# A transformer block with routed experts: thirteen filling products in each attention-only body of TensorE's program

## The reference, cut to what matters

```python
h = patches(x) @ W.T + b                       # 32 x 196 x 192
h = concatenate([h, txt], axis=1)              # 32 x 324 x 192
h = h + causal_attention_one_head_rope(layernorm(h), Wq, Wk, Wv)
n = layernorm(h)
y = n + proj(attention_12_heads(layernorm(n) * w + b))
logits = (layernorm(y) * w2 + b2) @ w_gate     # 8 experts, best 2 of them, softmax of the two
out = h + y + sum_over_experts(gate * (gelu(xn2 @ W1 + b1) @ W2 + b2))
```

## Time and profile before

| | |
|---|---|
| median of 3 runs | 2925.34 us (2924.81 to 2934.8) |
| the profiled execution | 2913.08 us |
| its span, first to last instruction | 2911.2 us |
| mean granted TensorE clock | 0.892 of full speed |
| PE busy | 2480.0 us, 85% of the span |
| VectorE busy | 1634.7 us, 56% |
| ScalarE busy | 1203.2 us, 41% |
| GpSimd busy | 785.4 us, 27% |

### The profile page before, as it was taken

How to read it: one execution, slowest core, us unless ns; L and a number is a source line. 1 busy time by engine, 2 the same in 40 slices (tenths; PEclk the granted TensorE clock), 3 DMA queues, 4 the chain that set the end, 5 groups by cost and what they waited for, 6 DMA issues and landing times.

```text
span 2911.2 us, 62705 instructions
## 1 busy us (share of the span) xinstructions
PE 2480.0 (85%) x19692; PEld 1930.7 (66%) x19692; DVE 1634.7 (56%) x3896; ACT 1203.2 (41%) x2270; POOL 785.4 (27%) x1003
## 2 busy tenths in 40 slices
PE   3888999999999998999999999999976788888600
PEld 3856666666666666777777777777756777777500
DVE  2358778887877877666666666666642111111133
ACT  2223343344334333565666666566652323333200
POOL 1113223323333332222222222222211121211265
PEclk9669789898989988999999999999999989889855
DMA  6513112211311224244444444444333666766533
GB/s 117 143 18 46 28 28 44 41 28 33 52 28 28 48 37 113 63 115 114 113 105 105 105 105 105 108 107 110 96 110 124 217 225 211 232 208 208 162 110 96
DMA packets 267172, 297.50 MB, mean 102 GB/s; under 512 B 36156, under 2 KB 235304, under 8 KB 267112
## 3 DMA queue, kind: packets, MB, share of 16 engines
q1 hardware_dynamic: 248680, 264.80, 36.4%
q0 software_dynamic: 18432, 31.93, 3.8%
HBM read 236.04 MB, written 60.55 MB: 102 GB/s over the span
## 4 chain that ended last, share of the span: by engine, by line
PE 72%; issue 7%; DVE 7%; DMA 5%; POOL 3%; ACT 3%; SPq 2%; DVEq 0%; ACTq 0%; POOLq 0%
PE PS L1590 45%; PE PS L1734 7%; PE PS L1745 6%; DMA B2t<-in_L_ffn_b 4%; PE PS L1661 3%; PE PS L1711 3%; POOL pool L826 2%; DVE MX L1258 2%; PE PS L1784 1%; DVE rsi L1270 1%; PE PS L1622 1%; PE PS L1672 1%; ACT XE L988 1%; ACT pool L968 1%; DMA pool<-ybuf,ydst 1%
## 5 line engine op out<-in xcount | busy, mean ns | idle before, releaser
L1258 DVE TENSOR_REDUCE MX<-PS 108x2 f32<-108x648 f32 x576 | 460.6, 825 | 87.0 <-PE PS L1711 81.0
L968 ACT ACTIVATE pool<-PS 108x648 f32<-108x648 f32 x576 | 389.9, 711 | 217.1 <-PE PS L1734 178.6
L1590 PE MATMUL PS<-WB,big 128*128 128x192 f32 x2304 | 428.8, 343 | 2.6 <-ACT big L997 2.6
L1590 PE MATMUL PS<-XE,WF 128*128 128x256 f16 x2880 | 365.9, 281 | 56.9 <-ACT XE L988 46.6
L1590 PEld LDWEIGHTS PS<-WB,big 128*128 128x128 f32 x2304 | 397.9, 201 | 17.2 <-issue 10.0
L997 ACT ACTIVATE big<-PS,WF 128x256 f32<-128x256 f32 x576 | 241.5, 470 | 361.6 <-PE PS L1590 360.9
L1590 PEld LDWEIGHTS PS<-XE,WF 128*128 128x128 f16 x2880 | 277.2, 100 | 122.6 <-ACT big L997 40.8
L1402 DVE TENSOR_TENSOR big<-PS,B2t 128x384 f32<-128x384 f32 x96 | 53.5, 557 | 530.2 <-PE PS L1590 530.1
L826 POOL DMA_INDIRECT pool<-ybuf,ydst x192 | 193.7, 1009 | 481.7 <-DVE pool L1425 321.1
L814 POOL DMA_INDIRECT xbuf<-XH,DST x192 | 192.4, 1002 | 230.6 <-DVE DST L1340 169.1
L1270 DVE RECIPROCAL rsi<-rsi 128x324 f32<-128x324 f32 x96 | 209.1, 2178 | 3.3
(11 more groups left out here) (207 smaller groups left out, 4254.3 us busy)
## 6 DMA issues: line engine op xcount, KB each, us to landing
WF<-w1p SPq DMA_DIRECT2D x96, 771.0 KB, 4.7
WB<-in_L_ffn_W SPq DMA_DIRECT2D x96, 576.0 KB, 5.7
ximg<-in_x SPq DMA_DIRECT2D x96, 196.0 KB, 5.0
ximg<-in_x SPq DMA_DIRECT2D x96, 195.1 KB, 8.4
Xt<-xbuf SPq DMA_DIRECT2D x96, 192.0 KB, 2.5
ybuf<-big SPq DMA_DIRECT2D x96, 192.0 KB, 5.8
B2t<-in_L_ffn_b SPq DMA_DIRECT2D x96, 96.0 KB, 6.0
rbuf<-RP SPq DMA_DIRECT2D x32, 248.1 KB
```

The lines of the kernel that those rows point to most:

```text
L968: nc.scalar.activation(Pr[:, at:at + 2, :], pair(("st", p))[0:TP, :, 0:T], ACT.Exp, scale=SCALE2).then_inc(S["ex"], 1)
L1258: nc.vector.tensor_reduce(MX[:, qt, g, 64 * jj:64 * jj + 64:32], pair(("s", p))[0:TP, :, 0:T], AX.X, ALU.max).then_inc(S["mx"], 1)
L1590: last = nc.tensor.matmul(out_ap, lhsT, rhs, start=(i == 0), stop=(i == len(products) - 1))
```

## The change

Each ATTEND body gets 13 more matmuls on PE, whose results nobody reads: 5 before `s1`, 3 before `pj`, 5 before `tr2`. Each has the 128 by 128 identity in fp16 as its weights and 512 columns of the first image weights (`attWa`, fp16) as the moving operand, and writes the first bank of the pair that the step is about to write. For that, the wait for the bank now comes first, then the fill, then the wait for the data. In BOTH bodies the two waits of these steps change places too, and nothing is filled. `tr1` stays as it was.

```diff
+            FILL = {("s1",): 5, ("pj",): 3, ("tr2",): 5}
+
+            def fill(turn, step, out_ap):
+
+                if turn.plan is ATTEND:
+                    for _ in range(FILL[step]):
+                        nc.tensor.matmul(out_ap, id16[:, :], attWa[:, 0, 0:512], start=True, stop=True)
...
             def turn_rows(turn, step, ready, b):
-                pe.wait_ge(S[ready], due(ready, b, 1))
-                free(pe, turn, step)
                 ps = pair(step)
+                if step in FILL:
+                    free(pe, turn, step)
+                    fill(turn, step, ps[:, 0, :])
+                    pe.wait_ge(S[ready], due(ready, b, 1))
+                else:
+                    pe.wait_ge(S[ready], due(ready, b, 1))
+                    free(pe, turn, step)
...
             def s1(turn, b):
-                pe.wait_ge(S["rs"], due("rs", b, 2))
                 free(pe, turn, ("s1",))
                 ps = pair(("s1",))
+                fill(turn, ("s1",), ps[:, 0, :])
+                pe.wait_ge(S["rs"], due("rs", b, 2))
...
             def pj(turn, b):
+                free(pe, turn, ("pj",))
+                fill(turn, ("pj",), pair(("pj",))[:, 0, :])
                 pe.wait_ge(S["no"], due("no", b, 3))
-                free(pe, turn, ("pj",))
```

## The result

The changed kernel takes 2940.89 us (median of 20 runs, 2930.62 to 2944.94) against 2933.98 (20 runs, 2924.06 to 2944.35) for the kernel before on the same chips. The ratio is 1.0028, 95% interval 1.0018 to 1.0038: "same" by the 0.5% of the forecast, and a hair slower. On the 2925.34 that stood ahead of the prediction this makes 2933.5, where 2927 was forecast with a range of 2889 to 2958. Three executions that stand far apart from the others of their kernel (5436.75 us of the kernel before, 3621.2 of e3, 9030.55 of e11) are left out of the ratios of the experiments.

What follows compares the result with a forecast made beforehand. PE was taken to bound the kernel, having lost clock in the ATTEND bodies. Delay +37 us and clock -35 us gave +2 us on the median 2925.34, so 2927 us ("same"), range 2889 to 2958.

Steps and rivals of the forecast that it cites:

- The delay, +37 us: Fills in 17 ATTEND bodies delay PE by 1.87 us each, 31.8 us, plus 5 us for `tr2` fills at half clock.
- its cover of 0.42: PE's 0.42 us of idle before `s1`, held to hide part of five fills of 1.08 us, so 0.66 show.
- The clock, -35 us: In the ATTEND bodies fewer falls raise PE's clock from 0.88 to about 0.93, a gain of 35 us.
- the 970 to 985: Sign of the forecast: the 17 ATTEND bodies sum to 970 to 985 us, at a clock of 0.92 to 0.94.
- a fall of 13.7 us: Stretch of 13.70 us with PE's clock at 0.5 behind the first scores, forecast to be gone after the change.
- this fall I hold for gone: Five fills before `s1` end the long half-clock stretch; seven bodies at 0.85 or lower then gain 22.6 us together.
- the 0.42 us of idle: PE's idle before `s1`; filling it with dense full-width work was the ground for ending the long half-clock stretch.
- the equal 2.65 us of busy time: Around the first scores, two bodies have equal PE busy time but only one loses clock: sign of being at the edge.
- The waits that change places ... that is nothing: Swapping bank and data waits costs nothing in BOTH bodies, as PE goes on at the later of the two.
- Faster, the falls nearly all go: Rival, chance 0.30: the ATTEND bodies reach a clock of 0.97, gaining 66 us less 32 of cost, 2891 us.
- Slower, the fills buy no clock: Rival, chance 0.30: the fall moves behind the scores, some fills run at half speed; +40 us, 2965 us.
- everything the change can win or lose lies in the 977: The 17 ATTEND bodies, 977.00 us in the profile before, were said to hold all possible gain or loss.

Runs made afterwards that it cites:

- e3: Changed kernel with only the five fills before `tr2`, none before `s1` and `pj`; ratio to the kernel before 1.0005.
- e11: Changed kernel with two fills before `s1`, one before `tr2`, `pj`'s waits as before the change, one wait per pair of banks; ratio to the kernel before 0.9753.
- e5: Changed kernel with its changed order of waits but no fills at all; ratio to the kernel before 0.9933.
- e1: Changed kernel with only the five fills before `s1`, none before `pj` and `tr2`; ratio to the kernel before 1.0019.
- e4: Changed kernel with two fills before `s1`, one before `tr2`, none before `pj`; ratio to the kernel before 0.9854.
- e6: Changed kernel with only two fills before `s1`, its order of waits kept; ratio to the kernel before 0.9929.
- e8: Changed kernel with two fills before `s1` and one before `tr2`, each on 32 rows in place of 128; ratio to the kernel before 0.9944.
- e12: Changed kernel with its 5, 3 and 5 fills on 32 rows of the array in place of 128; ratio to the kernel before 1.0260.
- e7: Changed kernel with only one fill before `tr2`, its order of waits kept; ratio to the kernel before 0.9869.

## Why the prediction was right, and where it was not

The forecast, "same", with 2927 us, holds: the measured +0.28% is +8 us where +2 was summed. That is partly luck. The order of waits, costed at nothing, is worth about -20 us (e5), and the fills with what they give back +28 (1.0028 against 0.9933) where +2 was summed; the two errors have opposite signs.

**The delay, +37 us: about right in sum.** At a clock of 0.91 a body is 58.0 us against 55.70, 2.3 x 17 = 39 us (the four bodies of before at 0.91 last 55.4 to 56.6). Its parts were not what was written. `s1` starts 0.82 us behind `rs` in place of 0.23: 0.59, forecast 0.66, and its cover of 0.42 was real. `pj` starts 0.79 behind `mx 3` at full clock (0.66 later, 0.65 fill), and 1.26 in the median body, since PE is at half clock there in most; only what `tr1` absorbs was taken off rightly. `tr2` starts 2.52 behind `n1` in place of 0.23, 2.29 later, forecast 0.81 and 1.07 more in five bodies: its fills run at half clock in every body. In the median body the three starts are 0.59 + 1.13 + 2.29 = 4.0 us later; what of that does not show in the 2.3 must be absorbed by later waits, and the sum agrees because parts taken too small and an absorption hardly counted cancel.

**The clock, -35 us: too much by the traces, near it by the medians, and from another source.** In the traces 0.88 rose to 0.91 and not to 0.93; 0.03 x 43 x 17 = 22 us, and the 17 bodies sum to 997.40 us, above the 970 to 985 that were to show the forecast. But the trace of before is of a fast execution: over the whole program it was granted 0.892, where the executions of that kernel beside e1 to e4 have a median of 0.887; those of the changed kernel have 0.8995, its trace 0.899. With a delay of 39 us and +8 measured, about 31 us must have come back in the median execution, an estimate from these two numbers. No body has a fall of 13.7 us left, as was held. But the reason given, the fill of the wait before the scores, is not the cause: those falls are gone without any fill (e5), and two fills there change nothing (e6), while with narrow fills there they are back (e8, e12). The step that failed is "this fall I hold for gone" with its ground, the 0.42 us of idle; the equal 2.65 us of busy time were a sign of how little decides, and with e5 a shift of tenths of a microsecond did. Why such a shift ends the falls stays open.

**"The waits that change places ... that is nothing": wrong.** The reasoning was that PE goes on at the later of two waits either way. In the bodies of the loop it goes on at the later of the two plus 0.08 to 0.10 us for each wait that stands behind it. That moved three steps by -0.17, -0.17 and +0.10, and alone gave 0.9933. Against that, the 13 fills as they are cost 1.0028 / 0.9933, nearly 1%. So the change is the sum of a gain that the forecast does not name and of a loss by its fills: one fill before `tr2` is worth 0.64%, thirteen as placed cost 0.95% (a comparison over two jobs).

**The rivals.** "Faster, the falls nearly all go" reckoned with bodies at 0.97. Its price of 43 per unit, carried on from 53.50 at 0.97, gives 52.2 for a body at 1.0, and e4 has 51.8. Its 2891 us was reached with one fill and with two and one (2890.93 in e7, 2887.36 in e4), not with thirteen. "Slower, the fills buy no clock" is nearest to e12, where the array was given less work; its price was forecast +40 us, and is +78 between the medians of that slower job. The 131 ns that the Trainium skill, "TensorE: Matmul & The Clock Gate", section "Back-to-back issue gap", gives as sustained spacing do not hold here: 217 ns stand between the fills at full clock. The Trainium skill's "TensorE: Matmul & The Clock Gate", section "A second HAM failure mode: psum-queue depth-cycling", which blames short idles between groups, is supported in part: removing tenths of idle did change the clock, but e8 and e12 filled the same idles with narrow work and it fell.

Three small readings of the prediction were off without bearing on the sum: "everything the change can win or lose lies in the 977" leaves out the last stretch, whose clock differs between traces; in the clock's row the third slice shows a 6 and the fifth a 7, not 8 or 9; and in the last ATTEND body PE waits 4.4 and 3.7 us, where the others have no wait over 0.6.

## What to carry to other kernels

In a loop, put the wait that ends last at the end of a step's waits, and wait once where two banks have one releaser: that was worth 0.7% here, and 1.8% in the slower job, in a kernel bound by PE, and needs no extra work. Start with no more products in a wait of PE than the wait is long, and measure each place by itself with the order of waits held fixed, since the pattern of clock falls answers to tenths of a microsecond and a gain or loss can come from the shift and not from the fill. A comparison of two single traces misleads here; the kernel before varied by 20 us over 20 executions, and its profiled one was shorter still.

## What the runs showed of the hardware that was not expected

In a loop a wait that is already met still costs PE 0.08 to 0.10 us when it stands behind one that has just ended (nine step starts in three kernels), and the trace shows an instruction of PE's queue for each; in the one body outside the loop this price does not show. The length of a body settles into a repeating cycle, and kernels of different work can settle at the same mean: 58.0 us with 5 fills before the scores or 5 before the second turning, 58.05 with all 13. And work of nearly equal length was not equal to the clock: with thirteen fills on 32 rows in place of 128 the first ATTEND body ran at 0.77 against 0.89, and with three at 0.79 against 0.95.
